# Gated attention's loop, a quantised linear layer and the front of a cross attention, written as one pipeline over groups of rows

## The reference, cut to what matters

```python
x = x + _L0_attn_ref(_layernorm(x), ...)        # gated linear attention, 16 heads
x = x + _L0_ffn_ref(_layernorm(x), weight, bias)  # quantised linear layer
x = x + _L1_xattn_ref(_layernorm(x), ctx_1024, ctx_1024, mask, ...)  # cross attention
# gated attention, at the end:
o = (o - o.mean(-1)) * rsqrt(o.var(-1) + EPS)   # per head
out = silu(g) * o @ Wout
# quantised layer: blocks of 32 features
scales = maximum(max(abs(blocks)) / 7.5, eps)
xd = nearest_on_grid(blocks / scales) * scales
out = xd @ wd.T + bias
# cross attention: q from x; k, v from the context of each batch
q = query @ Wq + bq;  k = key @ Wk + bk;  v = value @ Wv + bv
```

## Time and profile before

| what | value |
|---|---|
| median of 3 runs | 1320.3 us (1317.45 to 1321.52) |
| the profiled execution's own time | 1313.18 us |
| its span | 1311.9 us |
| busy over the span: PE, DVE, ACT, POOL | 94%, 56%, 39%, 11% |
| stage 2's loop, first mask to last statistics | 263.6 to 346.3 us |
| stage 3 | 347.2 to 403.4 us |
| front of stage 4, to the first scores | 404.4 to 448.5 us |

### The profile page before, as it was taken

How to read it: one execution, slowest core, us unless ns; L and a number is a source line. 1 busy time by engine, 2 the same in 40 slices (tenths; PEclk the granted TensorE clock), 3 DMA queues, 4 the chain that set the end, 5 groups by cost and what they waited for, 6 DMA issues and landing times. The chain is left out here.

```text
span 1311.9 us, 25872 instructions
## 1 busy us (share of the span) xinstructions
PE 1230.5 (94%) x11069; PEld 916.5 (70%) x11069; DVE 730.3 (56%) x1572; ACT 517.7 (39%) x1018; POOL 138.2 (11%) x158
## 2 busy tenths in 40 slices
PE   7999889989587999999999999999899999999999
PEld 4654468756235777777777777777688767887887
DVE  5467486546696455554545455555585745434342
ACT  3334448432003454455454445454453332222321
POOL 2300030335341300000000000000031100000000
PEclk9999999899888999999999999999999899999999
DMA  9769400000303211100010100001400200010200
GB/s 288 282 241 401 171 0 1 0 1 1 126 10 113 97 65 43 56 34 33 34 34 33 34 33 34 34 34 33 82 1 1 73 0 33 33 33 32 64 33 32
DMA packets 49335, 88.23 MB, mean 67 GB/s; under 512 B 19211, under 2 KB 20285, under 8 KB 45125
## 3 DMA queue, kind: packets, MB, share of 16 engines
q1 hardware_dynamic: 48160, 86.01, 19.1%
q10 hardware_dynamic: 1060, 0.56, 0.1%
HBM read 65.59 MB, written 20.97 MB: 66 GB/s over the span
## 5 line engine op out<-in xcount | busy, mean ns | idle before, releaser
L1856 ACT ACTIVATE K<-bank,vecT 128x512 f32<-128x512 f32 x64 | 44.1, 689 | 171.4 <-PE bank L256 171.4
L1871 ACT ACTIVATE W<-W,low 128x512 f32<-128x512 f32 x128 | 91.0, 713 | 46.8 <-DVE low L1775 46.8
L186 POOL TENSOR_TENSOR rstd<-rstd,half_pow 128x1 f32<-128x1 f32 x48 | 29.9, 629 | 699.0 <-DVE rstd L182 699.0
L1775 DVE CUSTOM_DVE_ANT_0 W<-bank,W 128x512 f32<-128x512 f32 x128 | 80.8, 688 | 40.0 <-PE bank L1644 40.0
L1753 DVE TENSOR_TENSOR W<-bank,vecT 128x256 f32<-128x256 f32 x16 | 6.8, 425 | 167.1 <-PE bank L1665 167.1
L256 PE MATMUL bank<-woT,hR 128*128 128x512 f32 x384 | 94.8, 403 | 2.3 <-DVE woT L273 2.3
L256 PE MATMUL bank<-xT,wT 128*128 128x512 f32 x384 | 94.8, 396 | 0.8 <-ACT W L2711 0.5
L256 PE MATMUL bank<-Wq,Wkv 128*128 128x512 f32 x384 | 93.0, 394 | 0.0
L256 PE MATMUL bank<-Wkv,ctxT 128*128 128x512 f32 x384 | 92.9, 394 | 0.0
L256 PE MATMUL bank<-ctxT,Wkv 128*128 128x512 f32 x384 | 92.5, 394 | 0.3 <-DVE ctxT L273 0.3
L256 PE MATMUL bank<-Wkv,Wq 128*128 128x512 f32 x384 | 92.4, 395 | 0.1
(11 more groups left out here) (350 smaller groups left out, 2230.3 us busy)
## 6 DMA issues: line engine op xcount, KB each, us to landing
W<-ctx_turned SPq DMA_DIRECT2D x16, 1024.0 KB, 4.8
W<-in_ctx_dram SPq DMA_DIRECT2D x8, 1024.0 KB, 10.7
ctx_turned<-ctxT SPq DMA_DIRECT2D x8, 1024.0 KB, 7.7
ctx_turned<-W SPq DMA_DIRECT2D x8, 1024.0 KB, 6.8
XT<-in_ctx_dram SPq DMA_DIRECT2D x4, 1024.0 KB, 11.0
XT<-in_L_ffn_wi_dram SPq DMA_DIRECT2D x4, 1024.0 KB, 6.1
XT<-in_L_ffn_wo_dram SPq DMA_DIRECT2D x4, 1024.0 KB, 5.1
raw_own<-in_ctx_dram SPq DMA_DIRECT2D x3, 1024.0 KB, 11.3
```

The costliest lines, as they stand in the source:

```text
L186: pool.tensor_tensor(rstd[:, g:g + 1], rstd[:, g:g + 1], half_pow[:], ALU.pow).then_inc(rstd_ok.s, 1)
L1775: dve.tensor_tensor_reduce(out=PR[:, j, :], in0=bank[:, 4 + j % 4, :], in1=mask, scale=1.0, scalar=3.0e38, op0=ALU.add, op1=ALU.min, accum ...
L1856: act.activation(K[:, m, :], bank[:, n % 4, :], ACT.Identity, bias=pcol("L1_xattn_bk", m)).then_inc(ring_a.s, 1)
L1871: act.activation(PR[:, j, :], PR[:, j, :], ACT.Exp, bias=low[:, j:j + 1], scale=-1.0, accum_out=total[:, j:j + 1]).then_inc(expd.s, 1)
```

## The change

The loop of stage 2, stage 3 and the front of stage 4 become one loop over t = 0 to 13. Stage 3 is no function of its own and works on single groups (128x512) instead of pairs. The two barriers go. Stage 4's front splits `Wkv` in eight pieces in iterations 0 to 3 (`key_weights_a`, `key_weights_v`), the context in iteration 10, `Wq` in 11 and 12; two key products end iterations 11 and 12 (`key_pe`), two stand between the transposes of stage 4. Centring moves behind all four masks. Stage 4's tiles get one map (`map_of_stages_4_and_5`), so that they can be written while stage 2 runs; q's two input halves no longer share memory with the context. SP's loads of stage 4's weights and first context move up into stage 2.

```diff
@@ SP, new in stage 2
+                sp.wait_ge(wt_v.s, wt_v(11))
+                load_slot(6, "L1_xattn_Wv")
+                sp.wait_ge(aug_pe.s, aug_pe(0))
+                load_slot(5, "L1_xattn_Wk")
@@ POOL's loop
+                for t in range(G + 7):
+                    if 5 <= t < G + 5:
+                        scale_pool(t - 5)
+                    if 7 <= t < G + 7:
+                        row_stats_pool(3, t - 7)
+                    if 5 <= t < G + 5:
+                        bias_pool(t - 5)
+                    if 4 <= t < G + 4:
+                        row_stats_pool(2, t - 4)
+                    if 1 <= t <= G:
+                        gated_pool(t - 1)
+                        deviation_pool(t - 1)
@@ PE
+            def turn_blocks_pe(g):
+                pe.wait_ge(scaled.s, scaled(g))
+                if g + 2 < G:
+                    pe.wait_ge(ynm.s, ynm(g + 2))
+                if g:
+                    pe.wait_ge(xt_a.s, xt_a(G + g - 1))
...
+            def linear_pe(g):
+                pe.wait_ge(xt_a.s, xt_a(G + g))
+                pe.wait_ge(xsum.s, summed(1, g + 2) if g + 2 < G else summed(2, g - 1))
...
@@ PE's loop
-                for t in range(G + 3):
+                for t in range(G + 6):
                     if 1 <= t <= G:
                         attend_pe(t - 1)
-                    if t >= 3:
+                    if 3 <= t < G + 3:
                         widen_pe(t - 3)
                     if t < G:
                         scores_pe(t)
+                    if 6 <= t:
+                        linear_pe(t - 6)
                     if 1 <= t <= G:
                         mean_of_pe(t - 1)
-                    if t >= 3:
+                    if 5 <= t < G + 5:
+                        turn_blocks_pe(t - 5)
+                    if 3 <= t < G + 3:
                         project_pe(t - 3)
                     if 1 <= t <= G:
                         variance_pe(t - 1)
+                    if t in (G + 3, G + 4):
+                        key_pe(t - G - 3)
@@ DVE's loop
-                for t in range(G + 4):
+                for t in range(G + 6):
                     if 3 <= t < G + 3:
                         normal_v(t - 3)
                     if t < G:
-                        masked_v(t, 0)
-                        masked_v(t, 1)
+                        for r in range(4):
+                            masked_v(t, r)
+                    if 6 <= t < G + 6:
+                        linear_v(t - 6)
                     if 1 <= t <= G:
                         centre_v(t - 1)
-                    if t < G:
-                        masked_v(t, 2)
-                        masked_v(t, 3)
-                    if t >= 4:
-                        stats_of_v(t - 4)
+                    if t < C:
+                        key_weights_v(t)
+                    if 4 <= t < G + 4:
+                        stats_of_v(1, t - 4)
+                        quantise_v(t - 4)
                     if 1 <= t <= G:
                         variance_v(t - 1)
                     if 3 <= t < G + 3:
                         add_v(t - 3)
+                    if t == G + 2:
+                        for c in range(C):
+                            context_v(c)
+                    if G + 3 <= t < G + 5:
+                        for c in range(2):
+                            query_weights_v(2 * (t - G - 3) + c)
+                    if 6 <= t < G + 6:
+                        stats_of_v(2, t - 6)
+                    if 7 <= t < G + 6:
+                        normalise(xn4, 3, t - 7)
@@ DVE, the split of the key and value weights
+            def key_weights_v(c):
+                for n in range(2):
+                    dve.wait_ge(wt_a.s, wt_a(12 + 2 * c + n))
+                    split_v(Wkv[:, 1, n, c, :], W[:, 5 + n, c, :], Wkv[:, 0, n, c, :]).then_inc(wt_v.s, 1)
@@ ACT's loop
-                for t in range(1, G + 3):
+                for t in range(1, G + 5):
                     if t <= G:
                         attended_a(t - 1)
                     if t + 1 < G:
                         sigmoid_a(t + 1)
+                    if t - 1 < C:
+                        key_weights_a(t - 1)
                     if 2 <= t < G + 2:
                         widen_a(t - 2)
                     if t <= G:
                         square_a(t - 1)
-            nc.all_engine_barrier()
...
+                    if t >= 5:
+                        blocks_a(t - 5)
```

More of the change, by code:

```diff
@@ L1008, in project_pe, with key_pe @@
                 ins.then_inc(proj.s, 1)
+            def turn_blocks_pe(g):
[5 more added lines that the diff above has]
+                for c in range(C):
+                    ins = pe.transpose(bank[:, 6, c * P:(c + 1) * P], xq[:, g, c * P:(c + 1) * P], ident[:])
+                ins.then_inc(turned.s, 1)
+            def linear_pe(g):
+                pe.wait_ge(xt_a.s, xt_a(G + g))
+                pe.wait_ge(xsum.s, summed(1, g + 2) if g + 2 < G else summed(2, g - 1))
+                for c in range(C):
+                    ins = pe.matmul(bank[:, 7, :], xd[:, g % 2, c * P:(c + 1) * P], slot(8)[:, c, :], start=(c == 0), stop=(c == C - 1))
+                ins.then_inc(proj.s, 1)
+            def key_pe(m):
+                if m == 0:
+                    pe.wait_ge(wt_v.s, wt_v(19))
+                    pe.wait_ge(ctx_v.s, ctx_v(C - 1))
+                product(bank[:, m, :], lambda h, c: Wkv[:, h, 0, c, m * P:(m + 1) * P], lambda h, c: ctxT[:, h, c, :],
+                        C).then_inc(ring.s, 1)
             def last_pe(g):
@@ L1332, in widen_a, with blocks_a, key_weights_a, query_weights_a @@
                          var[:, g % 2, :].unsqueeze(2).broadcast_to([P, GH, GDV])).then_inc(wide_a.s, 1)
+            def blocks_a(g):
+                act.wait_ge(turned.s, turned(2 * G + g))
+                if g >= 2:
+                    act.wait_ge(proj.s, proj(linear[g - 2]))
+                act.copy(xd[:, g % 2, :], bank[:, 6, :]).then_inc(xt_a.s, 1)
+            def key_weights_a(c):
+                for n in range(2):
+                    act.wait_ge(slot_in[5 + n].s, slot_in[5 + n](1))
+                    split_a(Wkv[:, 0, n, c, :], W[:, 5 + n, c, :]).then_inc(wt_a.s, 1)
+            def query_weights_a(c):
+                act.wait_ge(slot_in[2].s, slot_in[2]())
+                split_a(kept["Wq"][:, 0, c, :], W[:, 2, c, :]).then_inc(wt_a.s, 1)
+            def context_a(c):
+                act.wait_ge(raw_in.s, raw_in(0))
+                split_a(ctxT[:, 0, c, :], raw[:, c, :]).then_inc(ctx_a.s, 1)
             def scalar():
@@ L1500, in l0_quantised_linear @@
+                    if t >= 5:
+                        blocks_a(t - 5)
+                    if t == G + 2:
+                        for c in range(C):
+                            context_a(c)
+                    if t == G + 3:
+                        for c in range(C):
+                            query_weights_a(c)
             sync()
@@ L1701, in tensor @@
                         u += 1
-                pe.wait_ge(wt_v.s, wt_v(5))
-                for m in range(C):
-                    keys_pe(0, m)
                 for i in range(NI):
@@ L1786, in vector @@
                 for g in range(G):
-                    normalise(xn, 3, g)
-                for g in range(G):
                     for k, (high, low_half, src) in enumerate(views[g]):
```

353 lines of the change are left out of this document (153 added, 200 removed).

## The result

The changed kernel takes 1329.2 us (median of 5 executions, 1328.31 to 1333.72), the kernel before 1320.3 (5, 1317.45 to 1321.52): ratio 1.008, 95% interval 1.0057 to 1.0102. It is slower by 8.9 us. In this document an execution that stood more than 1.5% above the fastest of its kernel in its set is left out of medians and ratios; that was one, of the kernel with all edits (experiment 7).

What follows compares the result with a forecast made beforehand. The bound was taken to go PE, DVE, PE before, with DVE setting the merged loop's pace where there are masks. -1.9 us at full clock plus 7.0 for the clock gave +5 on the median 1320.3: 1325 us, range 1309 to 1336.

Steps and rivals of the forecast that it cites:

- Iterations 0 to 3: Masks of group 0 to group 4: DVE's splits wait for ACT's casts, 41.3 us against 30.5, 10.8 us lost.
- Iterations 4 to 11: Merged loop up to the last quantisation's end: DVE sets the pace where there are masks, 100.4 us in all.
- POOL and DVE: Quantisation in iterations 4 to 8: POOL's gated product slows DVE's chain by 0.9 us in each.
- The tail: Last quantisation's end to stage 4's first scores: scale, transposes, key and linear products, q products; scores start at 446.5, full clock.
- 10.7 until the q products: In the tail, PE transposes stage 4's groups with two key products among them and waits for DVE's splits: 10.7 us.
- The clock: PE's longer waits lower TensorE's clock in iterations 1 to 3, 5 or 6, and 9 to 11: 7.0 us charged.
- The sum: Whole change: -1.9 us at full clock plus 7.0 for the clock, +5 us, giving 1325 us.
- Cheap quantisation: Rival, DVE in iterations 4 to 11: single groups cost no more than pairs, POOL doesn't collide; 1314 us, chance 0.25.
- Cancels: Rival: the clock holds through the short waits, leaving -1.9 us, 1318 us, no change; chance 0.18.
- The clock falls at nearly every wait: Rival, PE's waits: low clock behind nearly all of them, +14 us, 1334 us; chance 0.17.
- The merge does what it says: Rival: PE's idle time of stage 3 disappears without DVE becoming the bound, -19 us or so; no chance given.

Runs made afterwards that it cites:

- experiment 7: Changed kernel with casts first, centring between masks, gated product first, unread matmuls in iterations 5, 9 to 11, second key product behind the last linear product: 1309.82 us.
- experiment 3: Changed kernel plus 19 matmuls of 128x512 that nobody reads, in PE's waits of iterations 1, 2, 5 and 9 to 11: 1319.03 us.
- Experiments 1 and 2: Changed kernel with all eight casts of Wkv ahead of iteration 1: 1321.35 us; changed kernel with DVE's splits one iteration later: 1321.16 us.
- experiment 4: Changed kernel with POOL's gated product ahead of its row statistics' power: 1325.43 us, ratio to before 1.0029.
- experiment 5: Changed kernel with all casts of Wkv ahead of iteration 1 and centring back between the masks in iterations 0 to 4: 1320.84 us.
- third set: Runs on another chip: the kernel before (1321.68 us, n 11) beside the all-edits kernel with keys as in the change, with and without unread matmuls (1308.97, 1310.02).
- the changed kernel again: The changed kernel with no edit, run again as the base beside the other runs: 1332.55 us, ratio to before 1.0082.
- experiments 8 and 9: Changed kernel with casts first, centring between masks, gated product first, unread matmuls in iterations 5, 9 to 11: 1308.97 us; then without unread matmuls: 1310.02 us.

## Why the prediction was right, and where it was off

1325 us was forecast with 1309 to 1336, slower 0.47; it came to 1329.2, slower. Point by point:

- **Iterations 0 to 3** were right in cause and size. At full clock the forecast was 41.3 us, measured 41.6 in experiment 3 (iterations of 9.4, 9.9, 11.1, 11.2; 8.7, 10.0, 11.25, 11.35 forecast; the first had low clock there too). Experiments 1 and 2 remove the wait in two ways and with it 11 us of time.
- **Iterations 4 to 11** from `normal_v` to the end of the last quantisation: 100.4 forecast. In experiment 3, where the clock held but for one place, 307.87 to 408.33 = 100.5, and no single iteration is off by more than 0.7. In the changed kernel 309.52 to 417.14 = 107.6. One sign was missed: DVE was to be busy over 90% in iterations 4 to 8 and was busy 76 to 91%, 78 to 91% in experiment 3 too; its waits for PE's products and for POOL's power held it up more than I had seen.
- **POOL and DVE:** the size, 0.9 a group, was right (1.49 - 0.55 = 0.94 in iterations 4 to 8), its place was not. I had drawn it from L235, which has two SBUF operands. The steps of the chain like it (L264 to L272, 0.69 each) ran when POOL was idle. What collided is the normalisation, with one full tile as input; experiment 4 shows the gated product to be the partner. That the size agrees although it was taken from another instruction is partly luck, and the right one stood in the trace of before: two normalisations took 1.00 us with POOL idle, 1.35 in the very row from which I measured a pair, and 1.78 with POOL adding the bias for most of it (380.73 to 383.22). The Trainium skill ("GPSIMD Engine Reference", "Key points") names contention for instructions in a 2-port mode of VectorE as well as for those with two SBUF inputs; I had used only the second half of that sentence. The trace agrees with it for two splits with two SBUF operands, 2.14 against 1.30 (below), and does not speak against it for the normalisation, 1.49 against 0.55; in which mode that ran no row tells. The two rows of the kernel before:

```profile
358.41 1.00 DVE L190 TENSOR_SCALAR xn<-X,mv,rstd 128x512 f32<-128x512 f32 x2
...
382.18 1.78 DVE L190 TENSOR_SCALAR xn<-X,mv,rstd 128x512 f32<-128x512 f32 x2
```

- **The tail** was forecast at 41.85; experiment 3 has 408.33 to 451.88 = 43.5. The term "10.7 until the q products" was 12.3 (416.59 to 428.88), the others hold within 0.3.
- **The clock** is the step that was mis-sized. I chose 7.0 of 0 to 16. The difference of the changed kernel to experiment 3 (one execution of each; what the unread matmuls themselves delayed is in it) gives it by parts: iterations 0 to 3 46.2 - 41.6 = 4.6 (3.3 forecast), 4 to 11 107.6 - 100.5 = 7.1 (3.7), tail 45.1 - 43.5 = 1.6 (0). Together 13.3 us, and the medians differ by 13.5. The error in the first two parts is one: I charged a low-clock product 0.9 to 1.1 us, but the clock stayed low through most of a product, or through several (L1111 1.7 to 2.5 us longer, L1093 1.7 and 2.5, and in iterations 1 and 2 attend, transposes and scores, one after another). The third is the key product at 419.11, 4.58 us instead of 3.01, to which I had charged nothing. The rule of the Trainium skill ("TensorE: Matmul & The Clock Gate", "A second HAM failure mode: psum-queue depth-cycling"), by which small idle times make the clock swing, told there of another kernel and without a price, was nearer to this than my middle value: here it swung in iterations 0 to 2, 4, 5 and 9 to 12.
- **The sum** for the stretch was -1.9 + 7.0 = 5.1; it is -1.9 + 2.1 (ledger: 0.3, 0.1, 1.7) + 13.3 = 13.5, the measured +13.5. The error in the time, 4 us, is smaller than 8.4: the profiled execution of before, whose stretch is the base here, lay 7.1 us under its median, that of the changed kernel on its median. How much of the 7.1 lay in the stretch was not measured. So the nearness of 1325 to 1329.2 is in part luck: the same two kernels in the next set differed by 12.6 us in their medians, not by 5.
- **Rivals.** Cheap quantisation: out, a chain was 4.8 (314.86 to 320.66 is 5.8, of it 0.95 the collision). Cancels: out for the change as made, but it is where experiments 1, 2, 3 and 5 end; experiment 3 is its very condition, a clock that holds, and ends at a ratio of 0.9979 (not apart from 1) and a stretch of 185.0 against 184.9. The clock falls at nearly every wait (+14, 1334): nearest in its term, 13.3 of 14, though not at nearly every wait. The merge does what it says (-19): out as made; with the order mended and unread matmuls the stretch fell by 13.6 us (184.9 to 171.3), some 70% of it, and the time by 1.05%.

## What to carry over

When stages are merged, work that was hidden in one place comes to stand in front of something on an in-order queue: for every consumer ask where its producer stands in the *other* engine's order, here a split in iteration t whose cast is behind the copy of t+1. A wait of a few us on PE can cost more than its length, in the work behind it: here 1.7 to 2.5 us for a product of eight 128x512, and some 3.2 for an iteration's small matmuls (experiment 5). Look at what work could stand in the wait. But clock is only worth having where PE's chain sets the end: in stage 3 of the kernel before, a product 1.9 us shorter did not bring the next transposes forward. And take several traces before a part of the stretch is compared.

## What the runs showed of the hardware

- Equal waits of PE do not give equal clocks. Behind 1.62 us the granted clock over the next 7 us was 1.00 in one kernel and 0.51 in another, with the same instructions on PE ahead. Behind 2.82 us in one execution it was low at once at 279.83, and at 290.58 full for 2 us and then low. That it isn't decided by the length of the wait alone is shown; what decides it stays open.
- The scatter of this kernel goes with the clock. In the third set the 11 executions of the kernel before reach from 1312.82 us at a mean granted clock of 0.979 to 1327.46 us at 0.969. A profiled execution can therefore lie 6 to 9 us beside its median (7.1 under for the kernel before, 6.4 over for the changed kernel again, 8.3 under and 8.6 over in experiments 8 and 9), as much as the change is worth, and a stretch from one trace is no measure of a difference of a few us.
- The normalisation of 128x512 (one full tile, two values per row) took 1.49 to 1.51 us beside POOL's product of 1.29 and 0.55 without: 0.94 lost, three quarters of POOL's own time. In iteration 11, two splits took 2.14 with POOL at work and 1.30 in iteration 0, and POOL's scale beside them 1.43 instead of 1.05. With the casts first (experiment 1) the splits of iterations 1 to 3 fell beside the gated product and took 2.38 to 2.40 for two, and the product 1.67 to 1.69.
